# One block for two stages, wider stores of Z, keys and queries, and an item's load ahead of the wait for the Gram stores

## What is computed

```python
x = embeddings[ids];  x = layernorm(x)
k, q, v = (short_conv(x @ W.T + b, conv) for each of the three)      # 4 taps
k, q = k / |k|, q / |q| per head;  v = silu(v);  b = sigmoid(x @ Wbeta.T) * k
# per sequence and head, chunk after chunk, W_t and W_avg being 16x16 states:
T    = tril(b_i @ k_i.T, -1);  inv = inverse(I + T)
U_i  = inv @ (eta * v_i - b_i @ W_t)
W_t  = W_t + k_i.T @ U_i           # and W_avg, a weighted mean of the states
O_i  = q_i @ W_avg * a + q_i @ W_t * c + (T_mat * (q_i @ k_i.T)) @ U_i
h    = x_embedded + rmsnorm(O) @ Wout.T + bout;  xn = layernorm(h)
y    = shared_swiglu(xn) + sum of the 2 best of 8 experts' swiglu(xn), weighted;  out = h + y
```

## Time and profile before

| what | value |
|---|---|
| median of 3 runs | 1499.73 us |
| time of the profiled execution | 1518.6 us |
| its span, first to last instruction | 1516.8 us |
| mean granted clock of TensorE | 0.874 of full |
| PE busy, DVE busy | 1179.7 us (78%), 764.9 us (50%) |
| queue q1 (all loads and stores of SP): packets, MB, share of 16 engines | 202944, 194.28, 45.3% |

### The profile page before, as it was taken

One profiled execution on the slowest core, in us unless ns is written; L12 is line 12 of the kernel. 1 busy time (PEld: TensorE's weight loads), 2 busy tenths in 40 slices (PEclk: granted clock), 3 DMA queues, 4 the chain that ended last, 5 costly groups with the idle time before them and its releaser, 6 DMA issues. The chain is left out here.

```text
span 1516.8 us, 28805 instructions
## 1 busy us (share of the span) xinstructions
PE 1179.7 (78%) x10846; PEld 791.1 (52%) x10846; DVE 764.9 (50%) x1707; ACT 515.8 (34%) x1049; POOL 388.6 (26%) x366
## 2 busy tenths in 40 slices
PE   4766456566656561688697987999999999999997
PEld 2543334353535351466475764555666666666664
DVE  4599849586868683567646873221111212121211
ACT  3454245353636360433243332331122222222221
POOL 6100113131202021513226003662022222222222
PEclk9788679777878785867888997999999999999999
DMA  7644566868585968777687747953122323232322
GB/s 269 188 101 134 120 178 142 251 140 248 128 255 121 259 136 235 199 224 224 179 246 225 230 152 278 377 171 103 32 40 46 48 45 49 44 49 43 49 44 31
DMA packets 237366, 228.68 MB, mean 151 GB/s; under 512 B 88980, under 2 KB 177972, under 8 KB 236080
## 3 DMA queue, kind: packets, MB, share of 16 engines
q1 hardware_dynamic: 202944, 194.28, 45.3%
q0 software_dynamic: 16368, 19.96, 7.5%
q10 hardware_dynamic: 17920, 12.59, 2.8%
HBM read 117.39 MB, written 115.62 MB: 154 GB/s over the span
## 5 line engine op out<-in xcount | busy, mean ns | idle before, releaser
L1644 DVE TENSOR_TENSOR hid_all<-p_s,silu 128x512 f32<-128x512 f32 x103 | 71.3, 692 | 378.8 <-PE p_s L1495 249.7
L1694 POOL DMA_INDIRECT out_h<-y_sb,x_in x71 | 110.6, 1558 | 360.9 <-DVE y_sb L1656 343.0
L1552 ACT ACTIVATE silu<-p_m 128x512 f32<-128x512 f32 x103 | 61.5, 597 | 328.0 <-PE p_m L1488 223.4
L804 DVE SCALAR_TENSOR_TENSOR cv<-raw,conv_sb,cv 128x512 f32<-128x512 f32 x144 | 117.5, 820 | 83.6 <-ACT raw L698 81.7
L175 DVE TENSOR_TENSOR xt<-xt,prod 128x62 f32<-128x62 f32 (+15 forms) x248 | 142.0, 572 | 4.3
L172 DVE TENSOR_TENSOR prod<-nx,xt 128x62 f32<-128x62 f32 (+15 forms) x248 | 138.4, 558 | 2.5
L1510 PE MATMUL p_y<-wo,hid_all 128*128 x568 | 134.4, 379 | 0.8 <-ACT hid_all L1569 0.8
L1488 PE MATMUL p_m<-wi,xT_c 128*128 x284 | 133.5, 592 | 0.5 <-ACT xT_c L1565 0.5
L1495 PE MATMUL p_s<-ws,xT_c 128*128 x284 | 133.6, 593 | 0.0
L288 PE MATMUL p_item<-xbd,bv_i 128*32 128x128 f32 x1024 | 46.8, 340 | 108.4 <-issue 39.5
L575 PE MATMUL p_p<-xT,wqkv_sb 128*128 128x512 f32 x192 | 108.6, 705 | 0.7 <-issue 0.7
(11 more groups left out here) (155 smaller groups left out, 2093.9 us busy)
## 6 DMA issues: line engine op xcount, KB each, us to landing
slots_in_dram<-xt SPq DMA_DIRECT2D x18, 520.0 KB
x_in<-slots_in_dram SPq DMA_DIRECT2D x71, 130.0 KB, 2.1
q_channels_dram<-qT SPq DMA_DIRECT2D x128, 64.0 KB
k_tokens_dram<-h SPq DMA_DIRECT2D x32, 256.0 KB
chunk_gram_dram<-h SPq DMA_DIRECT2D x32, 256.0 KB
beta_kv_dram<-h SPq DMA_DIRECT2D x8, 1024.0 KB
nx<-chunk_gram_dram SPq DMA_DIRECT2D x8, 1024.0 KB, 6.3
scores_dram<-h SPq DMA_DIRECT2D x8, 1024.0 KB
```

The costliest lines, as they stand in the source:

```text
L804: ins = dve.scalar_tensor_tensor(cv[:, p, m, :], raw[:, p, m, j:j + L], conv_sb[:, p, m, j:j + 1], cv[:, p, m, :], ALU.mult, ALU.add)
L1644: dve.tensor_tensor(dst, p_s[n % 2][:], silu[n % 2][:], ALU.mult).then_inc(S["hid_ready"], 1)
L1694: pool.indirect_dma_start(token_rows, bass.IndirectOffsetOnAxis(x_in[s % X_IN][:, D:D + 1].bitcast(U32), 0), y_sb[s % 2][:], None, compute ...
```

## The change

Six edits, all on the movement of data and on waits:

1. Stage one and stage two stand in one block. The meeting of the engines between them is gone; waits on single semaphores take its place (below).
2. The second stage's constants and the loads of its steps 0 and 1 (`start`) are issued in the first stage's last pass, after the first half of the Gram stores and ahead of the store of beta kv.
3. The queries of a sequence are stored by 8 stores of 128 KB in place of 16 of 64 KB. The array in DRAM is `[B, HQ, P, L]` instead of `[B, TILES, P, HQ, P]`, so a row written is 2 KB and was 512 bytes, and a row read by the load of `q_i` is 512 bytes and was 2 KB.
4. The keys of a sequence are stored by one store of 1 MB in place of four, Z and the inner part of an item by one of 256 KB in place of four of 64 KB. The arrays in DRAM are `[B, L, 2 * D]` instead of `[NC_BATCH, B, C, 2 * D]`, so the four sequences' rows that a step loads (`zo`, `kk_b`) no longer lie side by side: the load reads four pieces of 32 rows.
5. In the passes 2 to 6 the load of the next pass's second item and the store of Y of its first stand in front of the wait for the Gram stores, so ahead of `nx` and of the scores. They stood behind both.
6. The loads of item 0 stand in the middle of pass 2, ahead of the store of beta kv, and stood at its end.

```diff
-        qT_dram = nc.dram_tensor("q_channels_dram", [B, TILES, P, HQ, P], F32, kind="Internal").ap()
-        kk_dram = nc.dram_tensor("k_tokens_dram", [NC_BATCH, B, C, 2 * D], F32, kind="Internal").ap()
-        zo_dram = nc.dram_tensor("z_and_inner_dram", [NC_BATCH, B, C, 2 * D], F32, kind="Internal").ap()
+        qT_dram = nc.dram_tensor("q_channels_dram", [B, HQ, P, L], F32, kind="Internal").ap()
+        kk_dram = nc.dram_tensor("k_tokens_dram", [B, L, 2 * D], F32, kind="Internal").ap()
+        zo_dram = nc.dram_tensor("z_and_inner_dram", [B, L, 2 * D], F32, kind="Internal").ap()
...
         def load_scores(sp, r):
...
-            sp.dma_start(q_i[:], qT_dram[b, t]).then_inc(s_q_in, 16)
+            sp.dma_start(q_i[:], qT_dram[b, :, :, t * P:(t + 1) * P].rearrange("n p l -> p n l")).then_inc(s_q_in, 16)
...
         def store_rest(sp, r):
...
-            for c in range(CH):
-                sp.dma_start(zo_dram[t * CH + c, b], zo_out[i][tok(c)].rearrange("p w h d -> p (w h d)")
-                             ).then_inc(s_zo_st[i], 16)
+            sp.dma_start(zo_dram[b, t * P:(t + 1) * P], zo_out[i][:].rearrange("p w h d -> p (w h d)")).then_inc(s_zo_st[i], 16)
...
                     for b in range(B):
                         r = TILES * (b - AHEAD)
                         if b >= AHEAD:
-                            move_item(sp, r)
+                            if r:
+                                store_rest(sp, r - 1)
+                            load_scores(sp, r + 1)
                             move_item(sp, r + 1)
...
-                        for f in range(4):
-                            for m in range(2):
-                                for w in range(2):
-                                    sp.dma_start(qT_dram[b, :, f * C + w * DH:f * C + (w + 1) * DH, m::2].rearrange("t d n l -> d n t l"),
-                                                 qT[m * 4 * DH + f * DH:m * 4 * DH + (f + 1) * DH].rearrange("d n (t l) -> d n t l", t=TILES)
-                                                 ).then_inc(s_st, 16)
+                        for n in range(HQ):
+                            for w in range(2):
+                                sp.dma_start(qT_dram[b, n].rearrange("(f w d) l -> w f d l", w=2, d=DH)[w],
+                                             qT[n % 2 * 4 * DH:(n % 2 + 1) * 4 * DH, n // 2]).then_inc(s_st, 16)
...
+                            if half == 0 and b == B - 1:
+                                start_next(sp)
+                            if half == 0 and b == AHEAD - 1:
+                                load_x(sp, 0)
+                                load_scores(sp, 0)
...
+                        if AHEAD - 1 <= b < B - 1:
+                            load_x(sp, r + 5)
+                            store_y(sp, r + 4)
                         sp.wait_ge(s_ngst, 64 * (b + 1))
...
+            def start(sp):
+                sp.wait_ge(first["s_cv"], 6 * B)
...
+                load_step(sp, 0)
+                load_step(sp, 1)
...
                     sp.dma_start(zo[i][:].rearrange("p w d -> p (w d)"),
-                                 zo_dram[c, b:b + GROUP].rearrange("b i x -> (b i) x")).then_inc(s_zo[i], 16)
+                                 zo_dram[b:b + GROUP, c * C:(c + 1) * C]).then_inc(s_zo[i], 16)
...
+                        sp.wait_ge(s_kst, K_STORES * (b + GROUP))
                         sp.dma_start(kk[i][:].rearrange("p n x -> p (n x)"),
-                                     kk_dram[c, b:b + GROUP].rearrange("b i x -> (b i) x")).then_inc(s_kk[i], 16)
+                                     kk_dram[b:b + GROUP, c * C:(c + 1) * C]).then_inc(s_kk[i], 16)
...
+                pool.wait_ge(s_kst, K_STORES * B)
+                pool.wait_ge(first["s_bv"], 4 * B)
                 pool.memset(h[:, 0:4], 0.0).then_inc(s_hz, 1)
                 pool.wait_ge(s_hz, 1)
                 for n in range(4):
                     gather(n)
+                pool.wait_ge(s_st, STORES * B)
+                pool.wait_ge(first["s_ngst"], 64 * B)
                 pool.memset(h[:, 4:], 0.0).then_inc(s_hz, 1)
...
                 def grow(s):
...
                     pe.wait_ge(S["u_ready"], s + 1)
+                    if s == 0:
+                        pe.wait_ge(first["s_sT"], TILES * B)
...
                 pe.wait_ge(s_weights, 16 * 5)
+                pe.wait_ge(first["s_ktri"], TILES * B)
                 take_z(0)
```

More of the change, by code:

```diff
@@ L407, in build @@
[L407 to L423, removed]
-            s_rn = sem(ctx, "inverse_norms_ready")
-            s_nb = sem(ctx, "inverse_norms_spread")
+            s_ids, s_w, s_zero = (sem(top, n) for n in ("ids_in", "weights_in", "h_zeroed"))
+            s_emb = [sem(top, f"embedded{i}") for i in range(RING)]
@@ new lines, in sync @@
+            def sync(sp):
+                for s in range(NT):
+                    if s >= 2:
+                        load_step(sp, s)
+                    if s == 3:
+                        store_inverse(sp, B - 2)
+                    if s - 1 in item_in:
+                        r = item_in[s - 1]
+                        move_item(sp, r, more=r + 1 < ITEMS and r != BREAK)
+                    if s == 11:
+                        store_inverse(sp, B - 1)
+                        load_x(sp, BREAK + 1)
+                        load_scores(sp, BREAK + 1)
+                    if s == step_of[ITEMS - 1] + 2:
+                        store_rest(sp, ITEMS - 1)
@@ L960, in build @@
+            return dict(start=start, sync=sync, gpsimd=gpsimd, tensor=tensor, scalar=scalar, vector=vector)
+        with ExitStack() as ctx:
+            first = first_stage(ctx)
+        with ExitStack() as ctx:
+            second = second_stage(ctx)
             with nc.Block() as block:
@@ L993, in _ @@
-                    for s in range(NT):
-                        load_step(s)
-                        if s == 3:
-                            store_inverse(sp, B - 2)
-                        if s - 1 in item_in:
-                            r = item_in[s - 1]
-                            move_item(sp, r, more=r + 1 < ITEMS and r != BREAK)
-                        if s == 11:
-                            store_inverse(sp, B - 1)
-                            load_x(sp, BREAK + 1)
-                            load_scores(sp, BREAK + 1)
-                        if s == step_of[ITEMS - 1] + 2:
-                            store_rest(sp, ITEMS - 1)
+                    first["sync"](sp, second["start"])
@@ L1019, in _ @@
[L1019 to L1030 removed]
+                    first["gpsimd"](pool)
@@ L1226, in _ @@
-                    store_xnT(NT - 1)
-                    for i in range(2):
-                        act.wait_ge(s_xn_out[i], 16 * (NT // 2))
-                        act.wait_ge(s_xnT_out[i], 16 * (NT // 2))
+                    first["scalar"](act)
+                    second["scalar"](act)
                 @block.vector
                 def _(dve):
-                    link = Chain(dve, S["chain"], -1)
-                    dve.wait_ge(s_weights, 16 * 5)
-                    for k in range(KH):
-                        dve.tensor_scalar(wout_sb[:, k, :], wout_in[:, k, :], rms_sb[:, 0:1], None, ALU.mult).then_inc(s_wout, 1)
@@ L1338, in build @@
+                    second["vector"](dve)
         tail.close()
```

1536 lines of the change are left out of this document (784 added, 752 removed).

## The result

The changed kernel takes 1514.13 us (median of 7 runs, 1511.47 to 1521.6) against 1503.61 us for the kernel before on the same chip (median of 7). The ratio is 1.0081, 95% interval 1.0058 to 1.0105: slower by some 12 us (9 to 16). The prediction was 1514. The single terms behind it fit less well than the sum.

What follows compares the result with a forecast made beforehand. No engine was full in the first stage; the untouched third stage was PE-bound. Gains of 39.5 and 1.8 us against 55 lost gave +13.7 us: 1532 us as profiled, 1514 by the median, range 1450 to 1555.

Steps and rivals of the forecast that it cites:

- Each is dealt out by its outermost count, so to four engines: Query stores and zo, kk_b loads: outermost count 4 confines them to four engines; upper bound of cost, taken for the forecast.
- The first rival: All 16 engines carry the new transfers: 67 us gained, 1433 us; chance 0.17.
- 26 + 5 + 24 = 55 us: Second stage's loss on four engines: 26 us in 603 to 827 us, 5 in steps 16 to 20, 24 in last ten.
- "cheap" rival: Four engines at 23.5 GB/s or more each: plain step 7.6 us, total 1489 us; chance 0.26.
- The forecast sign: Last ten steps: u_out starts about 8.2 us apart instead of 5.8, PE waiting for zo or kk_b.
- 26 - 1.8 = 24: Up to step 16: 26 us lost to four-engine loads, less 1.8 us gained by one block through POOL's earlier scaling.
- 39.5 us gained: First stage: 17.5 us from edit 6, 4 from fewer stores, 4.5 from edit 5 in each of four passes.
- What is late next is DVE itself: Edit 6, pass 3: DVE's 17.55 us tap wait goes, then DVE's own work sets the pace; gain 17.5 us.
- 18 us were forecast in passes 4 to 7: Edit 5: PE's 7.41 us wait can go; 7 us per pass, 28 in all, cut to 4.5 per pass by backlog.
- What is late next are the second item's scores: Edit 5: after the moved load, these scores stand behind nx and the scores' store; still 7 us gained per pass before backlog.
- The 4 us of the saved issues in pass 4: Edits 3 and 4: fewer stores on SP, late itself in pass 4, remove DVE's 4.59 us wait; 4 us gained.
- the 25 that I had named as a sign of being wrong: First stage shortening by less than 25 us would mean the waits came back behind other loads.

Runs made afterwards that it cites:

- m1: Transfers alone, no layer computed: batches of 256 KB loads and stores, one side in 1 to 16 pieces; four-piece loads took 44.2 us, one-piece 13.7 us.
- e1: Changed kernel with the old DRAM layout of zo and kk (four stores each, loads in one piece): 1483.21 us, ratio to before 0.9873.
- e7: Kernel before with only zo and kk laid out as in the change, so loads read four pieces: 1539.25 us, ratio 1.0226.
- e3: Changed kernel with zo and kk_b loads in one piece and queries stored by 16 stores of 16x2x512: 1476.59 us, ratio to before 0.9833.
- e4: Kernel before, unchanged, profiled a second time: 1507.94 us.
- e6: Kernel before with edit 6 alone (item 0's loads in the middle of pass 2): 1492.99 us, ratio 0.9906.
- e5: Kernel before with edits 5 and 6 alone (both earlier loads): 1488.6 us, ratio 0.9891.
- e8: e3 with edit 5 taken back, so second item's load and first one's Y follow nx and scores: 1494.45 us, ratio to before 0.9863.
- e10: e3 with POOL's sum of item 20's queries ahead of the scores' store wait and blanking of h: 1476.9 us, ratio to before 0.9754.
- e2: Changed kernel with queries stored by 16 stores of 16x2x512, zo and kk_b still read in four pieces: 1511.73 us, ratio to before 1.0047.

## Why the prediction was right, and where it was not

**The mechanism.** "Each is dealt out by its outermost count, so to four engines" was taken against a lower bound of no cost, and it is what happened: m1 shows the share of 0.25, e1 and e7 that these loads alone turn a gain of 1.3% into a loss of 0.8%, and before into 2.3% slower. The first rival, 16 engines at 1433 us, is out. Even with all transfers on 16 engines (e3) the time is 0.9833 x 1503.6 = 1478 us, since the gains were overrated too. One reading in the prediction is wrong without changing it: of the outermost counts 32, 128 and 512, the orders shown have only 32 and 128; 512 is a row's length there.

**The second stage.** Forecast 26 + 5 + 24 = 55 us. Step 16 to 21 lost 5.2 (39.55 us from 782.21, and 34.4 in e4), as the term said. The last ten steps lost 16.3 (74.4 against 58.2), not 24. The term was mis-sized: 180 KB at 22 GB/s gave a step of 8.2 us, and 7.4 was measured. How much of this is the rate stays open. In m1 four engines did 23.8 GB/s each alone and 21.8 in the mixed batch, while 180 KB in a step of 7.1 us would be 25.4. The 7.6 us of the "cheap" rival fit no better for being near 7.4, since three of the steps were also long by a lower clock (last section). PE shows where the 16.3 us went: in these ten steps it is busy 64.0 us (55.7 in e4) and idle 10.5 (2.4 in e4). The forecast sign, PE waiting for `zo` or `kk_b`, came only in part. PE's matmuls wait 0.4 us for `zo` in all, and its weight loads 3.0. 5.1 us stand before `grow`, which reads `kk_b`, but the profile names nothing that ended them. 3.1 us are for `xnT`, and ACT in turn waited 7.1 us for the store of an earlier `xnT`, a wait that the forecast did not have:

```profile
872.33 0.37 ACT L1201 COPY xnT<-p_u_turn_x 128x256 f32<-128x256 f32 x1 [1.72 <-DMA ffn_input_channels_dram<-xnT]
```

From B to step 16 the loss is 9.3 us (245.1 against 235.8), and the forecast had 26 - 1.8 = 24: I stretched 166 us of DMA work to 229 without asking how much of it falls into steps of 10 to 15 us. From step 4 to 16 only 2.4 us are lost (146.0 against 143.6). I take it that the items and not the loads set the length there; no run isolates that. In all 31 us by the segments against 53; on 16 engines the same kernel would have gained there, so the loads' own price is rather the 31 to 34 us of the experiments.

**The first stage.** Forecast 39.5 us gained, 25.2 measured (A to B). The starts of the first beta-kv operation of each pass split A to B (us, one trace each):

| kernel | pass 2 to 3 | pass 3 to 7 |
|---|---|---|
| before (e4) | 82.9 | 312.1 |
| e6, edit 6 | 74.9 | 306.2 |
| e5, edits 5, 6 | 70.5 | 305.8 |
| after | 70.8 | 299.1 |
| e8, e3 - edit 5 | 75.3 | 302.5 |
| e3, all on 16 | 69.7 | 302.4 |
| e10, e3 + POOL first | 70.1 | 298.8 |

Edit 6 was near in size, 14 us by e6 for 17.5, but not in mechanism. "What is late next is DVE itself" is wrong: half of DVE's wait stayed, behind PE's wait for the second item's inverse, and the stretch from pass 2 to 3, where all the gain was forecast, is only 8 us shorter. Where the other 6 come from isn't shown. Edit 5 was wrong: 18 us were forecast in passes 4 to 7 (28 without the backlog). Adding it shortens the stretch from pass 2 to 3 by 4.5 to 5.6 us, which the forecast did not count, and the four passes behind by 0 to 4. "What is late next are the second item's scores" stood in the text, but I let that wait cost 2.5 us of 7, and PE's new wait is as long as the old one: the scores stand behind the same 2 MB as the load that was moved. The 4 us of the saved issues in pass 4 don't show either: DVE still waits 4.53 and 3.70 us at its taps there. Against the 22 us forecast for passes 4 to 7, after has 13.

**One block.** Step 0 starts 45 us earlier than in e4 (554.57 against 599.58), of which 25 are the first stage's. None of the other 20 is left at step 4. POOL's blanking was forecast to start over 20 us after DVE's last scores. It does, 30 us after (DVE's last scores end at 552.2 us). POOL in the changed kernel, then PE:

```profile
581.86 6.07 POOL L1030 MEMSET h<- 128x7168 f32 x1 [25.93 <-DMA scores_dram<-h]
```

```profile
567.59 1.93 PE L288 MATMUL p_item<-xbd,bv_i 128*32 128x128 f32 x32 [13.11 <-DMA xbd<-chunk_inverse_dram]
584.53 1.94 PE L288 MATMUL p_item<-xbd,bv_i 128*32 128x128 f32 x32 [4.58 <-DMA bv_i<-beta_kv_dram]
```

A place I had not seen is the first of PE's rows: item 20's load stands behind the loads of steps 0 and 1 on four engines, and PE waits 13.11 us for it; in e1, with these on 16, it is 8.15 us. With all transfers on 16 engines (e3) the stretch from B to step 4 is 6.4 us shorter than in e4 where I had allowed 1.8, so the block and the early start may bring something. It is little more than a trace resolves, though: e5 and e8 have 90.6 and 89.9.

**The sum.** I overrated the gain by some 14 us and the loss by some 22, so by the two profiles the kernel loses 6 us, and by the ratio of the runs 12, where I had 13.7; one profile of each is no finer than that. Both errors come from the same habit, taking a wait or a load at full price without its neighbours, and they partly cancelled. That the forecast of 1514 is met to the microsecond is an accident, and the sign is only in part the mechanism's doing. With the 41 us of gain that I forecast (39.5 + 1.8) and the measured price of 31 to 34, the kernel would have come out 7 to 10 us faster, near the 1489 us of the "cheap" rival. That rival was to decide when the second stage loses less than 41 us, and it lost 31; its time failed because the gains were smaller as well. The first stage's 25.2 us lie on the 25 that I had named as a sign of being wrong, and its waits did come back behind other loads. Not told apart by any run: what the saved issues of Z and k (edit 4's stores) and the queries' 2 KB rows bring by themselves. From e5 to e3, which adds the block, the early start and these rows, the ratio falls by 0.0058, with overlapping intervals.

## What to carry to other kernels

Read the outermost count of both sides of every transfer before changing a layout in DRAM: a store saved by merging pieces can put the load on the other side onto four engines, and here a pattern alone cost 34 us. In the profile it looks like a lower DMA share and fewer GB/s with longer steps. Where a load is moved ahead of a block of large transfers, list everything that stays behind it and that the same chain needs; the wait moves to the first of these at nearly full length. And a total that comes out right proves the terms only when each is measured.

## What the runs showed of the hardware that was not expected

- Four engines alone move 23.8 GB/s each over a batch of loads, sixteen 19.1 (m1), so confinement costs 3.2 times the time and not 4. Part of this is that the sixteen were busy for only 0.86 of their 13.7 us: while busy they moved 306 / (16 x 0.86) = 22.2. For stores it is 3.6 times, 23.5 against 341 / (16 x 0.92) = 23.2.
- Loads from 16 pieces of 8 rows kept a share of 0.90 but moved 234 GB/s; one piece had 0.86 and 306. Full width doesn't give the full rate: the same bytes took 17.9 us for 13.7.
- Where the waits were longer, the clock was also lower. From step 21 to 31 the granted clock was 0.91, 0.91 and 0.88 in the three kernels with four-piece loads (after, e2, e7), with PE idle 8.3 to 10.5 us, and 1.00 in e1, e3 and e4, with PE idle 2.4 to 2.5. In the step ahead of each fall of after PE was busy 5.8 to 5.9 us of 6.8 to 7.1, and in e4 5.6 of 5.8. That the waits brought the clock down is my reading; no run varied the waits alone. In the last nine steps of the changed kernel, cut at `u_out`, the six at a granted clock of 1.00 take 6.2 to 7.1 us, the three in which it fell 8.1, 9.6 and 8.3:

```profile
828.90:836.00 7.10, 5.85 (x113) 4.18 (x113) 4.87 (x18) 1.85 (x6) 0.00 (x0) 1.00 0.53 186
836.00:844.10 8.10, 7.12 (x113) 5.37 (x113) 4.95 (x19) 1.90 (x6) 0.00 (x0) 0.79 0.55 172
844.10:851.20 7.10, 5.93 (x113) 4.26 (x114) 4.83 (x19) 1.76 (x6) 0.00 (x0) 1.00 0.54 187
851.20:860.80 9.60, 8.62 (x113) 6.43 (x113) 4.88 (x19) 1.90 (x6) 0.00 (x0) 0.64 0.54 177
...
880.90:889.20 8.30, 7.35 (x114) 5.21 (x113) 4.92 (x19) 2.00 (x6) 0.00 (x0) 0.79 0.59 195
```

  Before, had 1.00 in such steps. Between the two levels of 1.2 and 2.4 GHz, PE's busy time in the slow step is 8.62 us where 5.85 does otherwise. Against the 7.1 us of their neighbours the three lost 1.0, 2.5 and 1.2 us, 4.7 in all. The step behind the slowest took 6.2 and so gave 0.9 back, which leaves an estimate of some 4 of the 16 us for the clock; a sum over the DMA queue alone doesn't hold them.
